# Mamba layers inside a one-core transformer kernel: a second VectorE tile and a lent PSUM bank in the narrow chunks, and the convolution's silu as one ScalarE call over four tiles

## The reference, cut to what matters

```python
def mamba_block(x, ip_w, cw, cb, xp_w, dtp_w, dtp_b, A_log, Dp, op_w):
    xz = jnp.einsum('bsd,ed->bse', x, ip_w)
    xi, z = jnp.split(xz, 2, axis=-1)
    xt = xi.transpose(0, 2, 1)
    conv = jax.lax.conv_general_dilated(xt, cw[:, None, :], (1,), [(DC_ - 1, 0)], feature_group_count=DI_) + cb[:, None]
    xi = jax.nn.silu(conv.transpose(0, 2, 1))
    xdbl = jnp.einsum('bse,fe->bsf', xi, xp_w)
    dt, Bm, Cm = jnp.split(xdbl, [DR_, DR_ + DS_], axis=-1)
    dt = jax.nn.softplus(jnp.einsum('bsr,er->bse', dt, dtp_w) + dtp_b)
    A = -jnp.exp(A_log)
    dA = jnp.exp(dt[..., None] * A)
    dBu = dt[..., None] * Bm[:, :, None, :] * xi[..., None]
    ... # h = dA * h + dBu along the positions, y = h . C, per channel and state
    y = ys.transpose(1, 0, 2) + xi * Dp
    y = y * jax.nn.silu(z)
    return jnp.einsum('bse,de->bsd', y, op_w)
```

## Time and profile before

| | |
|---|---|
| median of 3 runs | 4868.89 us (4865.0 to 4876.24) |
| the profiled execution, its own time | 4881.62 us |
| its span (first to last instruction) | 4879.8 us |
| busy share of the span: PE, DVE, ACT, POOL | 83%, 62%, 49%, 43% |
| mean granted TensorE clock, as a share of full speed | 0.936 |
| first to last Mamba scan | 1739.2 to 3842.7 us |
| instructions | 52253 |

### The profile page before, as it was taken

How to read it: one execution, slowest core, us unless ns; L and a number is a source line. 1 busy time by engine, 2 the same in 40 slices (tenths; PEclk the granted TensorE clock), 3 DMA queues, 4 the chain that set the end, 5 groups by cost and what they waited for, 6 DMA issues and landing times. The chain is left out here.

```text
span 4879.8 us, 52253 instructions
## 1 busy us (share of the span) xinstructions
PE 4046.8 (83%) x16840; PEld 2043.5 (42%) x16840; DVE 3037.8 (62%) x4016; ACT 2413.3 (49%) x4540; POOL 2115.1 (43%) x2146
## 2 busy tenths in 40 slices
PE   6987997898798688888888988888888686868687
PEld 3443443344344234444444444444444342424243
DVE  2543353273254159998899879997999562636353
ACT  2322331232232167777777777777777442424242
POOL 0210120030021058787788778886878530303121
PEclk9998998999999779999999999999999888888989
DMA  3000000000000223233232233222232100000000
GB/s 132 1 1 10 0 1 11 0 1 0 11 1 1 73 78 87 78 85 98 82 88 73 78 91 98 81 82 83 83 87 63 73 1 10 1 10 1 10 1 5
DMA packets 131774, 215.95 MB, mean 44 GB/s; under 512 B 18928, under 2 KB 118512, under 8 KB 124336
## 3 DMA queue, kind: packets, MB, share of 16 engines
q1 hardware_dynamic: 131216, 201.08, 14.4%
q0 software_dynamic: 288, 11.53, 0.6%
HBM read 186.26 MB, written 26.30 MB: 44 GB/s over the span
## 5 line engine op out<-in xcount | busy, mean ns | idle before, releaser
L1562 POOL TENSOR_TENSOR m_db<-m_u,m_bb 128x512 f32<-128x512 f32 (+1 forms) x1280 | 1463.1, 1164 | 453.8 <-DVE m_hh L1514 451.9
L1514 DVE TENSOR_TENSOR_SCAN m_hh<-psum,m_kept,m_db 128x512 f32<-128x512 f32 (+1 forms) x1024 | 1194.3, 1202 | 38.1 <-ACT m_kept L1334 23.4
L1313 ACT ACTIVATE psum<-m_dt,m_am 128x512 f32<-128x512 f32 (+1 forms) x1280 | 818.8, 643 | 329.1 <-DVE m_hh L1514 324.5
L1255 PE MATMUL psum<-cst,m_hh 128*128 128x128 f32 x4608 | 656.9, 282 | 225.9 <-ACT m_ys L1325 117.9
L1255 PEld LDWEIGHTS psum<-cst,m_hh 128*128 128x128 f32 x4608 | 520.4, 143 | 671.5 <-ACT m_ys L1325 258.1
L1263 PE MATMUL psum<-m_ys,cst 128*128 128x512 f32 x1280 | 672.8, 608 | 0.0
L620 POOL TENSOR_SCALAR a_pr<-a_pr,a_ri 128x512 f32<-128x512 f32 x256 | 173.9, 692 | 684.0 <-DVE a_ri L562 684.0
L1325 ACT ACTIVATE m_ys<-psum,m_bc 128x512 f32<-128x512 f32 x640 | 430.5, 673 | 31.0 <-PE psum L1255 29.5
L620 POOL TENSOR_SCALAR c_pr<-c_pr,c_ri 128x512 f32<-128x512 f32 x256 | 173.9, 692 | 578.4 <-DVE c_ri L562 578.4
L1528 DVE SCALAR_TENSOR_TENSOR m_yt<-psum,m_bc,m_yt 128x512 f32<-128x512 f32 x480 | 350.4, 730 | 64.5 <-PE psum L1255 64.4
L482 POOL TENSOR_TENSOR a_pr<-a_pr,a_ri 128x512 f32<-128x512 f32 x64 | 66.6, 1042 | 624.7 <-DVE a_ri L452 624.7
(11 more groups left out here) (212 smaller groups left out, 5958.8 us busy)
## 6 DMA issues: line engine op xcount, KB each, us to landing
m_bb<-b_rows SPq DMA_DIRECT2D x48, 1024.0 KB, 4.8
m_xr<-x_line SPq DMA_DIRECT2D x128, 192.0 KB, 3.9
m_bb<-b_rows SPq DMA_DIRECT2D x32, 768.0 KB, 4.3
m_xr<-x_line SPq DMA_DIRECT2D x128, 160.0 KB, 3.4
m_xr<-x_line SPq DMA_DIRECT2D x128, 128.0 KB, 3.1
m_xr<-x_line SPq DMA_DIRECT2D x128, 96.0 KB, 3.2
a_w1b<-w1b_in POOLq DMA_DIRECT2D x1, 7168.0 KB, 28.9
x_line<-m_xc SPq DMA_DIRECT2D x32, 192.0 KB, 4.4
```

What stands on the lines that cost most here:

```text
L1255: mm = nc.tensor.transpose(s[:, e * P:(e + 1) * P], hh[:, n % 2, e, t * P:(t + 1) * P], ident)
L1313: nc.scalar.activation(bank(DECAY[u % len(DECAY)])[:, 0:w], dt[:, g % 2, e, 0:w], ACT.Exp, scale=am[:, layer_of(g) % 2, e * DS + n:e * DS ...
L1514: nc.vector.tensor_tensor_scan(hh[:, n % 2, e, 0:w], bank(DECAY[u % len(DECAY)])[:, 0:w], db[:, u % 4, 0:w], kept[:, n, e:e + 1] if g % NI ...
L1562: nc.gpsimd.tensor_tensor(db[:, u % 4, 0:w], us[:, g % 2, e, 0:w], bb[:, at % 2, n % 4, 0:w], ALU.mult).then_inc(pool_done, pr.pool.step(f ...
```

## The change

Four things change in the Mamba part, and two places in the order.

1. `tiles_d` rounds up: in a 384 chunk DVE gets two turned tiles and ACT with PE one. PSUM bank 4 is then unused in such a chunk.
2. `SideBanks` replaces the ring of one side bank. A bank can be lent: bank 4 from q = 8 in the 384 chunks, banks 3 to 6 while item 0 is prepared alone, banks 0 to 2 while item 19 is finished.
3. The convolution's result is copied by ACT with its bias to SBUF, which frees the bank, and ACT's own Silu then runs once over all four tiles at q = `SILU` = 33. The four tanh on ACT, the four combining instructions on DVE and the halved bias on POOL go.
4. The places: `XD` 34 to 36, `DTP` 37 to 39, `BCT` 45 to 46, `SOFT` 45 to 47, `Z` two later, and the output product's first half from 58 to 33, its second from 61 to 60. When item 0 is prepared alone (`alone`), the z products come before the convolution.

```diff
 def tiles_d(g):
-    return list(range(width(g) // P // 2))
+    return list(range((width(g) // P + 1) // 2))
 def tiles_p(g):
-    return list(range(width(g) // P // 2, width(g) // P))
+    return list(range((width(g) // P + 1) // 2, width(g) // P))
+class SideBanks:
+    def __init__(self, prog, view, home):
+        self.prog, self.view, self.home, self.lent, self.emptied = prog, view, home, (), {}
+        self.order = []
+    def lend(self, banks, emptied):
+        for b in banks:
+            self.emptied[b] = emptied
+            if b in self.order:
+                self.order.remove(b)
+        self.lent = tuple(banks)
+    def take(self, job, steps, emptied):
+        fresh = [b for b in (*self.home, *self.lent) if b not in self.order]
+        k = fresh[0] if fresh else next(b for b in self.order if b in self.home or b in self.lent)
+        if k in self.order:
+            self.order.remove(k)
+        self.order.append(k)
+        freed, self.emptied[k] = self.emptied.get(k), (steps.sem, steps.at(emptied))
...
-            VAR, IN, YF, CONV, XD = 1, (6, 8, 10, 12), (14, 16, 18, 20), (22, 25, 28, 31), 34
-            DTP, BCT, SOFT, OUT, Z = 37, 45, 45, (58, 61), (46, 49, 52, 55)
+            VAR, IN, YF, CONV, SILU, XD = 1, (6, 8, 10, 12), (14, 16, 18, 20), (22, 25, 28, 31), 33, 36
+            DTP, BCT, SOFT, OUT, Z = 39, 46, 47, (33, 60), (48, 51, 54, 57)
+            SPARE_SUM = 8
...
-            sides = Ring(pr, bank, list(SIDES))
+            sides = SideBanks(pr, bank, SIDES)
...
+            first_z, past_z = Z[0], Z[-1] + 3
+            alone = [*range(0, IN[-1] + 2), *range(first_z, past_z), *range(IN[-1] + 2, first_z),
+                     *range(past_z, NE * DS)]
...
-                        b, freed = sides.take(f"{g} conv {e}", pr.dve, f"{g} xi {e}")
+                        b, freed = sides.take(f"{g} conv {e}", pr.act, f"{g} conv {e} out")
...
-                            pe.wait_ge(dve_done, pr.dve.at(f"{g} xi {NE - 1}"))
+                            pe.wait_ge(act_done, pr.act.at(f"{g} xi"))
...
-                    for q in range(NE * DS):
+                    spare = (*SUMS, TURN_D, TURN_P)
+                    sides.lend(spare, None)
+                    for q in alone:
                         side(q, None, 0)
...
+                            if len(tiles_p(g)) == 1 and NE * n + e == SPARE_SUM:
+                                k = len(tiles_p(g - 1)) - 1 if g else 0
+                                sides.lend(SUMS[1:], (act_done, pr.act.at(f"{g - 1} sum 1 out")) if k else sides.emptied[SUMS[1]])
+                            if n == 0 and e == 0:
+                                sides.lent = ()
...
+                    sides.lend(DECAY, (dve_done, pr.dve.at(f"{ITEMS - 1} scan {LAST} {NE - 1}")))
                     for q in range(NE * DS):
                         side(q, ITEMS - 1, None)
...
-                                nc.scalar.activation(xi[:, g % 2, j, 0:w], s, ACT.Identity, scale=0.5,
-                                                     bias=half_bias[:, j:j + 1])\
+                                nc.scalar.activation(xi[:, g % 2, j, 0:w], full(f"{g} conv {j}")[:, 0:w], ACT.Identity,
+                                                     bias=vec2(g, "cb", j))\
                                     .then_inc(act_done, pr.act.step(f"{g} conv {j} out"))
-                                act.wait_ge(act_done, pr.act.n)
-                                nc.scalar.activation(s, xi[:, g % 2, j, 0:w], ACT.Tanh)\
-                                    .then_inc(act_done, pr.act.step(f"{g} tanh {j}"))
...
+                        if q == SILU:
+                            act.wait_ge(act_done, pr.act.at(f"{g} conv {NE - 1} out"))
+                            nc.scalar.activation(xi[:, g % 2, :, 0:w], xi[:, g % 2, :, 0:w], ACT.Silu)\
+                                .then_inc(act_done, pr.act.step(f"{g} xi"))
...
-                            if q == CONV[e] + 2:
-                                dve.wait_ge(act_done, pr.act.at(f"{g} tanh {e}"))
-                                nc.vector.scalar_tensor_tensor(xi[:, g % 2, e, 0:w], full(f"{g} conv {e}")[:, 0:w], 1.0,
-                                                               xi[:, g % 2, e, 0:w], ALU.add, ALU.mult)\
-                                    .then_inc(dve_done, pr.dve.step(f"{g} xi {e}"))
```

24 lines of the change are left out of this document (12 added, 12 removed).

## The result

The changed kernel takes 4889.95 us (median of 9 runs, 4884.97 to 4901.52), the kernel before 4868.89 in the same series: ratio 1.0043, 95% interval [1.0033, 1.0052]. It is 21 us slower; 11 us faster was forecast, and the range ended at 4882.

What follows compares the result with a forecast made beforehand. DVE was taken to bound the items of 512, while most items of 384 had idle DVE time. Terms -7 + 9.6 - 7 - 5 = -9.4 us, with 1.5 more about -11, gave 4858 us against 4868.9; range 4832 to 4882.

Steps and rivals of the forecast that it cites:

- items of 512, silu and places, 12 of them: Items of 512 positions: DVE work saved against burst and gather waits, -1.8 us a layer, -7 us for four layers.
- item 19: Last item, no convolution to save on: the added tile lengthens it from 74.7 to 84.3 us, +9.6 us.
- items 4, 9, 14: 384 items: the added tile outweighs shrinking idle time, 96.9 against 94.8 us, three times +2.1, +6.3 us.
- items 5, 10, 15: 384 items: the added tile partly fills DVE's idle time, 99.9 against 102.0 us, three times -2.1, -6.3 us.
- prologue: Preparing item 0 alone: z products moved ahead and freer banks bring the first scan to 1732 from 1739.2, -7 us.
- finish: After the last scan: one ACT tile instead of two saves about 3.5 us, more banks 1.5, together -5 us.
- gathered rows: Convolution's late tiles: removed DVE work mostly becomes longer waiting for the gather, 1.3 us given back in items 1 and 2.
- a share of 1.5 us for the whole kernel: Extra gain for POOL's halved bias, ACT without tanh, and small waits at q = 37 and 39: 1.5 us together.
- The burst's own term: Silu call with two table loads on ACT: DVE waits 2.2 us in items 1 and 2, against 2.4 us saved.
- Rival (A): Burst digs deeper than softplus, PE and ACT come back late: 1.6 us more in all 19 items, 4888 us; chance 0.13.
- Rival (B): Each table switch costs twice its load: 38 more times 1.28 us, +49 before cover, 4907 us; chance 0.03.
- Rival (C): Relieved 384 items fall to DVE's need, item 4 to 93.3 us, item 5 to 94.6: about 4825 to 4832; chance 0.18.

Runs made afterwards that it cites:

- e9: e3 with the changed kernel's places, first output product at 33, without the Silu call or added tiles: 4894.19 us, ratio 1.0037.
- e17: The changed kernel with the old tanh and combining instructions in place of the Silu call, everything else kept: 4889.29 us, ratio 1.0032.
- e5: The changed kernel with its Silu call made a tanh call, so the two table loads go (another function is computed): 4860.05 us, ratio 0.9975.
- e6: The changed kernel with x_proj reading the previous item's convolution output from item 3 on, issued one step earlier: 4878.16 us, ratio 1.0011.
- e15: e14 with the changed kernel's Silu call instead of the tanh and products, no added tile: 4892.79 us, ratio 1.0041.
- e7: The changed kernel with the first output product back at step 58 and the second at 61: 4983.49 us, ratio 1.0224.
- e3: The kernel before with only the two stretches that run alone changed (lent banks, z products before the convolution), B/C turn at 44: 4859.51 us, ratio 0.9971.
- e2: The changed kernel without the Silu call and with the old places (B and C rows turned at 44): 4875.05 us, ratio 1.0003.
- e8: The changed kernel with the added tiles undone and the side bank not lent in 384 chunks: 4906.5 us, ratio 1.0072.
- e13: e3 with the first output product at steps 32 and 33, its residual at 34, nothing else moved: 4949.13 us, ratio 1.0157.
- e14: e3 with x_proj, dt, B rows, softplus and z each one step later, output product left at 58 and 61: 4861.94 us, ratio 0.9982.
- e10: e3 with an unused one-column Silu on ACT at step 33 of every item, adding two table loads: 4860.47 us, ratio 0.9975.
- e1: The kernel before with the Silu call and the new places, but old tiles and old ends: 4923.04 us, ratio 1.0115.

## Why the prediction was wrong

Sum by sum, from the traces and those above:

| term | forecast | measured |
|---|---|---|
| items of 512, silu and places, 12 of them | -7 | +21.6 |
| item 19 | +9.6 | +9.4 |
| items 4, 9, 14 | +6.3 | +0.5 |
| items 5, 10, 15 | -6.3 | -3 |
| item 0 | 0 | -1.2 |
| prologue | -7 | -11.6 |
| finish | -5 | -5.6 |

The measured column adds up to +10 us, the difference of the medians is +21; the rest is where the two profiled executions lie (see below).

For a layer's three items of 512, from DVE's timelines (us, means of four layers; the forecast's terms are put where they belong):

| | forecast | measured |
|---|---|---|
| DVE's busy time | -6.6 | -5.3 |
| its waits up to q = 32 (gathered rows) | +2.6 | -0.3 |
| its waits at q = 33 to 43 (5.8 for the burst, less 1.7 for residuals in its gap) | +4.1 | +11.2 |
| its waits from q = 44 on (softplus, second residual) | -1.9 | -0.2 |
| sum | -1.8 | +5.4 |

**The step that failed** is in the working of the silu's burst, where it prices what stands around the call: one wait right behind the burst, and "The first residual of the output product now runs inside the new gap, 0.6 us that cost nothing." It looked at DVE's residual and left out what the residual waits for. The move sends eight matmuls, twice four in 1.9 us at full clock, to steps 33 and 34, through the only side bank and ahead of the turned tiles, and puts `x_proj` right behind them; and the burst, which `x_proj` waits for, makes this `x_proj` late once more. The only thing counted for 37 and 39 was a share of 1.5 us for the whole kernel. What the runs showed in its place is DVE's waits at q = 33 to 43 (us):

| kernel | k1 | k2 | k3 | a layer |
|---|---|---|---|---|
| before | 0.8 | 0.8 | 0.0 | 1.6 |
| e9, new places, no call | 2.3 | 3.1 | 2.2 | 7.6 |
| e17, the same with tiles | 2.3 | 3.1 | 2.2 | 7.6 |
| e5, new places, call without loads | 2.5 | 3.8 | 1.0 | 7.3 |
| e6, changed, `x_proj` free | 3.4 | 4.7 | 1.0 | 9.1 |
| changed | 5.9 | 4.8 | 2.1 | 12.8 |
| e15, call, product late, rest one later | 3.7 | 3.6 | 1.7 | 9.0 |
| e7, changed, product late | 7.1 | 7.0 | 4.6 | 18.7 |

The new places bring about 6 us a layer, with or without the call and the tiles; the two loads bring another 5.5. In exchange the call saves 5.3 us of DVE's work. By the medians the places cost 32 us without call and tiles (e9 against e3), 14 without the call and with tiles (e17 against e2), and with the call and without tiles 15 (e8 against e15, whose other places are one step later and not at the old ones). I had even counted the move as a gain of 0.5 us in items 2 and 3, for a residual that no longer waits; it waits at 35 instead (item 3: 1.8 us for residuals in e9, 1.5 in e3), and the turned tiles behind it wait too. How much of the places' price is the product and how much `x_proj` is not shown: e13 (the product alone, one step further than in e9) and e14 (the rest alone, by one step instead of two) point at the product. And with the call, putting the product back late does little: the waits from 58 on are 5.2 us a layer in e15 and 1.6 in the changed kernel, which takes back nearly all that the table shows for it; only k1 is shorter in e15 (112.5 us against 115.7).

**The burst's own term** (+2.2 against -2.4 of DVE's work in items 1 and 2) had the call and loads right. The wait right behind it at 36 is 1.6 us in item 6 and 0.7 in item 2, less than the 2.2 taken from the softplus, because the output product has already made DVE late: with the product at 58 it is 3.2 us (item 7 of e7). What it left out is the wait at 39: 2.0 us in item 2, 1.2 in item 3, and 3.7 in items 6, 11 and 16, where PE's half clock through `x_proj` came on top, which no row of before showed at that place. With the product early, the call with its loads is worth -0.5 us a layer in the three items of 512 (e17), where -1.8 was forecast for it and the places together.

**Rival (A)** ends at the measured time, 4888, and its mechanism is there: PE and ACT do come back late together behind the call, and `x_proj` is late by it (e6, 16 us). But it priced the burst alone, in all 19 items; e17 shows the same time without any burst, and the new places have no part in (A). That its sum meets the time is luck in part, and it would be wrong to call (A) confirmed.

**Rival (B)** is out: loads and call follow each other directly in the rows above, and 39 loads more in e10 cost nothing. The Trainium skill, "ScalarE: Activation LUTs", section "What ACT_TABLE_LOAD costs", gives a drain beside each load; in the rows above 0.01 and 0.02 us lie between load, call and load, so no row there has room for one.

**Rival (C)** did not happen as such: item 4 takes 94.9 us, not 93.3, and item 5 101.6, not 94.6; the wait at 33 for the gathered rows' tile grew from 5.6 us to 6.3, so the tile's relief fell into it, as the forecast had said. In items 4, 9 and 14 I had counted 2 us too much each: DVE's busy time rose by 7.4 us in item 4 and its idle time fell by 7.3, so the length stood.

**The ends.** The prologue gained 4.6 us more than forecast. The rows there were at half clock (4 matmuls in 2.93 us); put back to back, the input and z products reached full clock, and the window's granted clock rose from 0.52 to 0.67. PE of the changed kernel:

```profile
1671.18 12.28 PE L1172 MATMUL psum<-m_xn,m_wa 128*128 128x384 f32 x32 [3.61 <-DVE m_xn L1515]
1683.38 0.85 PE L1195 MATMUL psum<-m_xr,m_dcw 128*32 128x384 f32 x8
```

All 32 matmuls take 12.28 us, eight times 2.93 would be 23.4. A forecast that took over their durations had to be too long. How much of the gain is the clock and how much the waits for banks that went was not separated.

**Profile against median.** From one profiled execution to the other the sum of -11 us came out as +4 (4881.62 to 4885.73), from median to median as +21. Neither profile lies at its kernel's median, and only the medians have an interval.

**Open.** Why the tiles and the lent bank make the new places cheaper (e17 against e9: 2 us less, although item 19 takes 7 more) was not separated into tile and bank. Why PE's clock fell behind 1.95 us of idle time in items 6, 11 and 16 of the changed kernel and not in items 1 and 6 of e1 was not found. No kernel was run in which the output product lies between 35 and 57, and none in which `x_proj` alone moves.

## What to carry to other kernels

When a change moves a step, cost everything the step issues on every engine, and follow the one buffer it passes through: a product that costs nothing to its own consumer can stand ahead of the work that everybody waits for. A hand-made order in which one buffer serves in turn has its places tied to each other; moving four of them by two forced the fifth, and the new places together were about half of the price. Two changes that each cost can cost less together than their sum, when one stall covers the other (e7): ask that of every pair. Undo a change's parts one by one before believing the part with the large, visible new instructions.

## What the runs showed of the hardware

- A pair of table loads around a call of 0.2 us (2.8 us of ACT in each of twenty items) did not change the time (0.9975 in e10 and 0.9971 in e3); the same loads around a call of 1.91 us, for whose output other engines wait, cost 33 us (changed kernel against e5).
- The four matmuls of `x_proj` took 3.60 us at a granted clock of 0.51 and 1.92 us at 1.00; the slow ones came right after PE had idled 1.95 us (items 6, 11 and 16), the fast ones after 0.27, 0.79 or 1.10 us. But in items 1 and 6 of e1 the same four came in 1.92 us after 1.95 us of idle time, so that idle time does not decide it alone. With `x_proj` issued into the idle stretch (e6), items 6, 11 and 16 went from 115.4 to 111.9 us.
- While item 0 was prepared, eight products (32 matmuls) issued back to back took 12.28 us; spaced by waits, each four of them had taken 2.93 us. The granted clock of that stretch was 0.67 instead of 0.52, and it ended 11.6 us sooner.
